# Turning x instead of its outer product, and loading the spherical rows repeated over the partitions, in a two-layer graph kernel

## The reference, cut to what matters

```python
def tensor_product(x_e, sh, w, C):
    # out[e,o] = w[e,o] * sum_{d,s} x_e[e,d] * sh[e,s] * C[d,s,o]
    acc = sh[:, 0:1] * (x_e @ C[:, 0, :])
    for s in range(1, S):
        acc = acc + sh[:, s:s + 1] * (x_e @ C[:, s, :])
    return acc * w
k = tensor_product(x_dst, edge_sh, wk, Cqk).reshape(-1, H, DQK)
v = tensor_product(x_dst, edge_sh, wv, Cv).reshape(-1, H, DV)
attn = jnp.einsum('ehd,ehd->eh', q[edge_src], k)
# softmax of attn over the edges of a node, then the weighted sum of v
```

## Time and profile before

| | |
|---|---|
| median of 3 runs | 3733.17 us |
| profiled execution | 3729.88 us, span 3728.2 us |
| PE / PEld busy | 3330.0 us (89%) / 3178.9 us (85%) |
| DVE busy | 2877.5 us (77%) |
| POOL busy | 2055.4 us (55%) |
| ACT busy | 1285.0 us (34%) |
| DMA queues q1, q0, q10 | 44.2%, 9.7%, 4.1% of 16 engines' span |

### The profile page before, as it was taken

One profiled execution on the slowest core, in us unless ns is written; L12 is line 12 of the kernel. 1 busy time (PEld: TensorE's weight loads), 2 busy tenths in 40 slices (PEclk: granted clock), 3 DMA queues, 4 the chain that ended last, 5 costly groups with the idle time before them and its releaser, 6 DMA issues. The chain is left out here.

```text
span 3728.2 us, 86642 instructions
## 1 busy us (share of the span) xinstructions
PE 3330.0 (89%) x25947; PEld 3178.9 (85%) x25947; DVE 2877.5 (77%) x5292; ACT 1285.0 (34%) x3333; POOL 2055.4 (55%) x1999
## 2 busy tenths in 40 slices
PE   2099999999999337999999999999999999999963
PEld 1088888888888237999999999999999999999953
DVE  4366666666666227999999999999999999999943
ACT  1033333333333113444444444444444444444420
POOL 2577777777777435555555555555555555555540
PEclk9599999999999658999999999999999999999975
DMA  8399999999999313444444444444444444444420
GB/s 339 86 268 280 279 279 279 279 280 279 279 280 279 105 46 105 127 126 132 131 124 129 131 129 124 130 132 126 125 132 132 124 128 131 130 124 129 132 78 29
DMA packets 843789, 622.16 MB, mean 167 GB/s; under 512 B 490431, under 2 KB 732803, under 8 KB 843452
## 3 DMA queue, kind: packets, MB, share of 16 engines
q1 hardware_dynamic: 667110, 500.09, 44.2%
q0 software_dynamic: 56640, 87.65, 9.7%
q10 hardware_dynamic: 119982, 33.79, 4.1%
HBM read 335.87 MB, written 286.31 MB: 167 GB/s over the span
## 5 line engine op out<-in xcount | busy, mean ns | idle before, releaser
L1305 POOL DMA_INDIRECT xg<-h_tab,src_i x808 | 861.5, 1066 | 220.8 <-issue 127.2
L789 POOL DMA_INDIRECT kv<-kv_tab,src_i x808 | 762.1, 943 | 285.7 <-issue 188.2
L1315 POOL TENSOR_TENSOR kq<-kvs,q_of 128x512 f32<-128x512 f32 x202 | 260.6, 1290 | 837.7 <-DVE kvs L1491 837.7
L1401 ACT ACTIVATE z_hi<-bank 128x512 fp32r<-128x512 f32 x808 | 439.4, 595 | 802.9 <-PE bank L1333 802.9
L1357 PE MATMUL bank<-C_hi,z_hi 128*128 128x256 f32 x4040 | 682.2, 299 | 0.0
L1357 PE MATMUL bank<-C_lo,z_hi 128*128 128x256 f32 x4040 | 612.2, 281 | 0.0
L1481 DVE TENSOR_TENSOR z_lo<-bank,z_hi 128x512 fp32r<-128x512 f32 x808 | 520.5, 686 | 113.5 <-ACT z_hi L1401 113.4
L1357 PEld LDWEIGHTS bank<-C_hi,z_hi 128*128 128x128 f32 x4040 | 537.8, 191 | 0.3
L1357 PEld LDWEIGHTS bank<-C_lo,z_hi 128*128 128x128 f32 x4040 | 535.3, 188 | 0.0
L1357 PE MATMUL bank<-C_hi,z_lo 128*128 128x256 f32 x3232 | 516.2, 281 | 0.0
L913 DVE TENSOR_TENSOR wsb<-bank,b 128x512 f32<-128x512 f32 x404 | 279.3, 691 | 298.7 <-PE bank L977 298.3
(11 more groups left out here) (248 smaller groups left out, 4754.4 us busy)
## 6 DMA issues: line engine op xcount, KB each, us to landing
w_tab<-wsb SPq DMA_DIRECT2D x202, 512.0 KB, 3.4
win<-w_tab SPq DMA_DIRECT2D x202, 512.0 KB, 3.6
sum_edge<-rowt SPq DMA_DIRECT2D x202, 288.0 KB, 2.5
q_edge<-zq SPq DMA_DIRECT2D x202, 256.0 KB
qs<-q_edge SPq DMA_DIRECT2D x202, 256.0 KB, 2.8
sum_edge<-rows ACTq DMA_DIRECT2D x202, 136.0 KB
qs<-q_edge SPq DMA_DIRECT2D x202, 128.0 KB
drow<-dst_tab SPq DMA_DIRECT2D x202, 128.0 KB, 3.2
```

Source lines behind the costliest of these rows:

```text
L789: pool.indirect_dma_start(kv[b][:, q, :], None, kv0_tab, bass.IndirectOffsetOnAxis(ap=src_i[:, i * Q + q:i * Q + q + 1], axis=0))\
L1305: pool.indirect_dma_start(xg[b][:, q, :], None, h1_tab, bass.IndirectOffsetOnAxis(ap=src_i[:, i * Q + q:i * Q + q + 1], axis=0))\
L1315: pool.tensor_tensor(kq[:, :].rearrange("p (q o) -> p q o", q=Q), kvs[b][:, :, 0:O1], q_of[b % 2][:, :].rearrange("p (q o) -> p q o", q=Q) ...
L1401: nc.scalar.activation(z_hi[b % 2][:, k, :], bank[ZB[k]][:, :], ACT.Copy).then_inc(hi_out, 1)
```

## The change

z is formed with features on partitions from the start. POOL gathers x as before; PE turns x alone (2 transposes per chunk instead of 18); ACT copies it to `xT`, where partitions 0 to 63 and 64 to 127 both hold the 64 features of all 512 edges. Since z then lies with (s,d) on partitions, sh must lie as one row of 512 edges for each s, repeated over 64 partitions. The middle phase therefore makes two tables, `sh_tab` (202 chunks x 8 x 512) and `sh_last_tab` (202 x 512), and in the second pass a DMA loads a chunk's rows repeated: 128 partitions with 8 KB each. Of the four pairs of sh, DVE multiplies three (one instruction of 1536 columns) and POOL the fourth (`z_part`). ACT and DVE then make `z_hi` and `z_lo` from SBUF in pieces of 1024 columns. `spread_q` gets a PSUM bank of its own.

```diff
             with nc.Block() as block:      # middle phase
+            SG = NST // 2                  # 101
+            sh_rows = [sb(f"sh_rows{g}", [SG, ST, S], F32, ph) for g in range(2)]
+            sh_parts = sb("sh_parts", [SG, S, ST], F32, ph)
                 def _(sp):
+                    def load_sh_rows(a):
+                        last_full = (NST - 1) * ST
+                        sp.dma_start(sh_rows[0][:, :, :], a[0:SG * ST, :].rearrange("(p e) s -> p e s", p=SG))\
+                          .then_inc(sh_rows_in, 16)
+                        sp.dma_start(sh_rows[1][0:NST - 1 - SG, :, :],
+                                     a[SG * ST:last_full, :].rearrange("(p e) s -> p e s", e=ST)).then_inc(sh_rows_in, 16)
+                        sp.dma_start(sh_rows[1][NST - 1 - SG:NST - SG, 0:TAIL, :], a[last_full:E, :].unsqueeze(0))\
+                          .then_inc(sh_rows_in, 16)
                     load_last_rows(sp, lrows, sum0_edge, last_got)
+                    with sp.If(flag > 0):
+                        load_sh_rows(ea9_s)
+                    with sp.Else():
+                        load_sh_rows(ea9)
...
                     sp.dma_start(car[:, :, :], ...).then_inc(car_got, 16)
+                    for g in range(2):
+                        sp.wait_ge(sh_parts_set, g + 1)
+                        sp.dma_start(sh_tab[g * SG:(g + 1) * SG], sh_parts[:, 0:S - 1, :]).then_inc(sh_put, 16)
+                        sp.dma_start(sh_last_tab[g * SG:(g + 1) * SG, :], sh_parts[:, S - 1, :]).then_inc(sh_put, 16)
                     sp.wait_ge(h1_ready, 1)
...
                 def _(act):                # after the copies to crows, ahead of those to wvT
+                    act.wait_ge(sh_rows_in, 48)
+                    for g in range(2):
+                        if g:
+                            act.wait_ge(sh_put, 32)
+                        for r in range(2):
+                            nc.scalar.activation(sh_parts[:, 4 * r:4 * r + 4, :],
+                                                 sh_rows[g][:, :, r:S - 1:2].rearrange("p e c -> p c e"), ACT.Copy)
+                        nc.scalar.activation(sh_parts[:, S - 1, :], sh_rows[g][:, :, S - 1], ACT.Copy)\
+                                 .then_inc(sh_parts_set, 1)
...
                     def load_sh(it, i, b):       # second pass, SP
-                        need(sp, z_ready, (i - RING + 1) * 2)
-                        load_either(sp, sh_turn, flag, i, sh[b][:, :, :], ea9, ea9_s, sh_in[b], sh_tail)
+                        need(sp, z_last_ready, i - 1)
+                        sp.dma_start(sh_last[b % 2][:, :], sh_last_tab[bass.ds(i, 1), :].rearrange(
+                            "a (r e) -> (a r) e", r=2).unsqueeze(1).broadcast_to([2, D, ST // 2])).then_inc(sh_in[b % 2], 16)
+                        need(sp, z_part_ready, i - 1)
+                        sp.dma_start(sh[b % 2][:, :, :].rearrange("p c e -> p (c e)"),
+                                     sh_tab[bass.ds(i, 1)].rearrange("a (r c) e -> (a r) (c e)", r=2)
+                                     .unsqueeze(1).broadcast_to([2, D, 4 * ST])).then_inc(sh_in[b % 2], 16)
...
+                    def z_part(it, i, b):        # POOL
+                        pool.wait_ge(x_out, i + 1)
+                        pool.wait_ge(sh_in[b % 2], 32 * (2 * it + b // 2 + 1))
+                        need(pool, lo_out, i * 3 - 4)
+                        pool.tensor_tensor(z[b % 2][:, ZD, :], xT[b % 2][:, :], sh[b % 2][:, ZD, :], ALU.mult)\
+                            .then_inc(z_part_ready, 1)
-                    unrolled([(times_q, -1), (gather_x, 4)], RING)
+                    unrolled([(times_q, -1), (z_part, 2), (gather_x, 5)], RING)
...
-                    pipelined(pe, [(t_z(0), 1), (t_z(1), 1), (turn_max, -2), (sums, -3), (m_acc(0), 0), (t_z(2), 1),
-                                   (t_z(3), 1), (m_acc(1), 0), (t_z(4), 1), (spread_q, 0), (m_acc(2), 0),
-                                   (turn_logits, -1), (m_acc(3), 0)], RING)
+                    pipelined(pe, [(turn_x, 3), (turn_max, -2), (sums, -3), (m_acc(0), 0), (m_acc(1), 0), (turn_logits, -1),
+                                   (spread_q, 0), (m_acc(2), 0), (m_acc(3), 0)], RING)
...
+                    def outer(it, i, b):         # DVE
+                        dve.wait_ge(x_out, i + 1)
+                        dve.wait_ge(sh_in[b % 2], 32 * (2 * it + b // 2 + 1))
+                        need(dve, lo_out, i * 3 - 4)
+                        dve.tensor_tensor(z[b % 2][:, 0:ZD, :], bcast(xT[b % 2][:, :], 1, ZD), sh[b % 2][:, 0:ZD, :],
+                                          ALU.mult).then_inc(z_ready, 1)
...
-                    pipelined(dve, [(product(1), -1), (lo(0), 1), (lo(1), 1), (subtract, -2), (outer(0), 2), (lo(2), 1),
-                                    (lo(3), 1), (logits, -1), (weigh, -2), (outer(1), 2), (lo(4), 1), (build, 1),
-                                    (segment_max, -1), (product(0), 0)], RING)
+                    pipelined(dve, [(product(1), -1), (subtract, -2), (outer, 2), (logits, -1), (weigh, -2), (lo(0), 1),
+                                    (lo(1), 1), (outer_last, 2), (build, 1), (lo_last, 1), (segment_max, -1),
+                                    (product(0), 0)], RING)
```

More of the change, by code:

```diff
@@ L1111, in _ @@
                     sp.wait_ge(tab3, 16)
+                    sp.wait_ge(sh_put, 64)
                     sp.wait_ge(carry_zero, 16 * 9)
@@ L1212, in gnn @@
             RING = 4
-            sh = [sb(f"sh{b}", [P, Q, S], F32, ph) for b in range(RING)]
+            sh = [sb(f"sh{b}", [P, 4, ST], F32, ph) for b in range(2)]
+            sh_last = [sb(f"sh_last{b}", [P, ST // 2], F32, ph) for b in range(2)]
+            xT = [sb(f"xT{b}", [P, ST], F32, ph) for b in range(2)]
             xg = [sb(f"xg{b}", [P, Q, D], F32, ph) for b in range(RING)]
@@ L1403, in stage @@
[L1403 to L1408 removed]
+                            nc.scalar.activation(z_hi[b % 2][:, 2 * k:2 * k + 2, :], z[b % 2][:, 2 * k:2 * k + 2, :],
+                                                 ACT.Copy).then_inc(hi_out, 1)
@@ L1409, in take_q, with hi_last @@
+                        return stage
+                    def hi_last(it, i, b):
+                        act.wait_ge(z_last_ready, i + 1)
+                        need(act, a_mm, i * 2 - 2)
+                        for f, e in zip(rows_of, edges_of):
+                            ins = nc.scalar.activation(z_hi[b % 2][f, 4, e], z_last[b % 2][f, :], ACT.Copy)
+                        ins.then_inc(hi_out, 1)
                     def take_q(it, i, b):
@@ new lines, in outer, with outer_last @@
+                    def outer(it, i, b):
[4 more added lines that the diff above has]
+                                          ALU.mult).then_inc(z_ready, 1)
+                    def outer_last(it, i, b):
+                        need(dve, lo_out, i * 3 - 3)
+                        for f, e in zip(rows_of, edges_of):
+                            ins = dve.tensor_tensor(z_last[b % 2][f, :], xT[b % 2][f, e], sh_last[b % 2][f, :], ALU.mult)
+                        ins.then_inc(z_last_ready, 1)
@@ L1481, in stage, with lo_last @@
-                            dve.tensor_tensor(z_lo[b % 2][:, k, :], bank[ZB[k]][:, :], z_hi[b % 2][:, k, :].bitcast(F32),
+                            c = slice(2 * k, 2 * k + 2)
+                            dve.tensor_tensor(z_lo[b % 2][:, c, :], z[b % 2][:, c, :], z_hi[b % 2][:, c, :].bitcast(F32),
                                               ALU.subtract).then_inc(lo_out, 1)
                         return stage
+                    def lo_last(it, i, b):
+                        dve.wait_ge(hi_out, i * 3 + 3)
+                        need(dve, a_mm, i * 2 - 2)
+                        for r in range(2):
+                            f, g, e = rows_of[r], rows_of[1 - r], edges_of[r]
+                            ins = dve.tensor_tensor(z_hi[b % 2][g, 4, e], z_last[b % 2][f, :],
+                                                    z_hi[b % 2][f, 4, e].bitcast(F32), ALU.subtract)
+                        ins.then_inc(lo_out, 1)
```

127 lines of the change are left out of this document (52 added, 75 removed).

## The result

The changed kernel takes 7142.83 us (median of 4 runs, 7138.11 to 7144.25) where the kernel before, run beside it, takes 3733.63 us (4 runs, 3731.1 to 3735.28): a ratio of 1.913, 95% interval 1.9097 to 1.9163. The forecast was 7240 us.

What follows compares the result with a forecast made beforehand. The prediction took the load of sh on two DMA engines, 27.4 us per chunk, to bound the second pass. 3729.9 + 16 + 3371 + 15 + 130 = 7262 us, forecast as 7240 us, range 6880 to 7700.

Steps and rivals of the forecast that it cites:

- The count of engines: Load of sh: engines are the largest number up to 16 dividing both sides' outer size, here two.
- The step: Second pass: sh packets plus a share of other transfers on two engines take 27.4 us per chunk; 201 steps, +3371 us.
- the rest of the queue: Second pass: each of the two engines also carries its sixteenth of other transfers, q1's 3.6 us and q0's 0.5.
- My doubt: Load of sh: an 8 KB packet read again and again may cost other than one read once, priced at 318 ns.
- Everything else hidden under it: Second pass: the two engines never run dry, so PE, DVE (9.7 us), POOL and ACT hide under them.
- The ends of the pass: Second pass: +16 us until the first outer product, and +15 us for the tail, from between 0 and 27.
- The middle phase: Table building: DMAs of 101 rows, a prime, run on one engine and delay ACT's wvT to about 1429; +130 us.
- the upper bound: Middle phase: strided reads double ACT's copies, making it +140 us.
- The sum: Whole kernel: 3729.9 + 16 + 3371 + 15 + 130 = 7262 us; 7240 forecast for packets at their lower price.
- Rival 1: Second pass: load spread over 16 engines, GpSimd and VectorE block each other; step 11.65 us, 4070 us; chance 0.06.
- Rival 2: Second pass: load spread over 16 engines, no blocking of long instructions; DVE bounds at 9.7 us, about 3545 us; chance 0.04.
- rival 3: Second pass: two engines per load, but successive loads take different pairs; 16 us a step, 4960 us; chance 0.04.

Runs made afterwards that it cites:

- distinct: dup_x, but the two sh loads read 64 differing rows of 8 KB each instead of one row 64 times; 3676.82 us, ratio 0.985 to the kernel before.
- mid_only: The kernel before with only the changed kernel's middle phase added, its tables written but never read; 3867.53 us, ratio 1.036.
- halves: The changed kernel with each load of sh and sh_last cut into two DMAs of 64 partitions; 4021.51 us, ratio 1.077 to the kernel before.
- z_on_dve: halves_mid with GpSimd's product z_part given to VectorE, as one outer product of 2048 columns; 3913.81 us.
- psum_x: z_on_dve with the outer product reading x from PSUM, table and gather holding x twice, ACT's copies dropped; 3728.29 us, ratio 0.9969 to the kernel before.
- halves_mid: halves with the middle phase in groups of 112 and 90 chunks instead of twice 101; 3896.44 us.
- dup_x: psum_x with gathers of 64 numbers again, ACT doubling the gathered rows in SBUF; 3683.9 us, ratio 0.985 to the kernel before.

## Why the prediction was right, step by step

**The count of engines.** Right, and the step on which all else hung. The completions show two engines for sh and two for sh_last, and in the variants 2, 3, 7 and 16. The Trainium skill ("DMA: Bandwidth & Descriptors", section "Why a DMA increments its semaphore by 16 and not by 1") has this rule; by it every count in the table comes out, and the trace agrees in all six. For the load of sh alone it shows in its 8 KB packets, of which two are under way at once and hardly ever three.

**The step: 27.4 us forecast, 26.83 measured.** The sum was 0.57 us too long, which makes 114 us over 201 steps. Which term that belongs to depends on how the 8 KB packet is counted. It was put at 318 ns, drawn from packets of 6400 and 14400 bytes. Its median is 309: 64 of these are 0.58 us less, and the rest of the queue, 3.6 + 0.5 = 4.1 us, is what the measured step then leaves (26.83 - 19.78 - 2.94 = 4.11). Its mean is 321, near the forecast, and then the rest was over-priced, with 3.35 us left for it. The trace doesn't name the engines, so it doesn't decide between the two. The 1 KB packet is 46 ns in the median, as worked out. My doubt that a packet that is read again and again has another price is answered by these 309 ns, which lie under what rows read once had suggested, and for sixteen engines by `distinct`.

**Everything else hidden under it.** Right. PE, VectorE, GpSimd and ACT each end in the wait for sh, and as far as the packets tell the two engines never ran dry: from the tenth to the ninetieth in a hundred the steps lie between 26.6 and 27.1 us. The granted clock was 0.69 and not the 0.5 that I allowed for.

**The ends of the pass.** 16 + 15 us forecast, 19.1 - 1.9 measured. The tail's 15 was the middle of a range of 0 to 27 and should have been its lower end; why it costs nothing was not looked into.

**The middle phase: +130 forecast, +134.0 measured**, and the same +134.0 alone in `mid_only`. Within it the load landed at 1332.6 (I had 1327), and ACT's two large copies took 7.54 us instead of 3.7: the doubling that I had put into the upper bound was what happened. The first store still kept its dates, because `car` and the zeros stood before it on its engine: its first packet is at 1353.9 us (I had 1350), and ACT goes on behind it and its companion at 1423.6 (I had 1423). `wvT` came 3 us later than 1429, by ACT's longer second copies.

**The sum.** 7262 us was added up and 7240 named, for packets at their lower price. The profiled run is 7138, 124 under the sum: 114 in the steps, 14 at the ends, and 4 the other way in the middle phase. No large errors cancelled.

**Rival 1**, had the load been spread, said 11.65 us a step and 4070 us. `halves` is that case: 11.37 and 4021.5. The wait for logits was priced at 1.3 us and is 1.2; `va`'s at 0.65 and is 0.45. **Rival 2** (9.7 us, no blocking) and **rival 3** (other pairs for successive loads) are excluded, the one by z_on_dve and psum_x, the other by steps of 26.83 and not 16 us and by the two packets under way. The Trainium skill ("SBUF — State Buffer", section "Who interferes with whom") speaks of an exclusive lock between a VectorE instruction with two SBUF inputs and GpSimd's reads; k x q at 2.83 us beside such an instruction and at 1.30 beside one that reads PSUM agrees with it.

## What to carry to other kernels

Before a broadcast load or a layout of tables is chosen, write down the outermost size on both sides of the DMA and the largest number up to 16 that divides both: in every kernel here that many engines carried it, and when they were too few, the rest of the queue waited for them. A mean DMA share tells nothing of this; the time of one packet times the packets per engine does, and so does the count of completion packets. Once that is right, look at which of VectorE's long instructions have both inputs in SBUF while GpSimd computes, and at how near the DMA engines' work per step is to the step.

## What I had not expected of the hardware

- The queue's issue itself takes longer when engines are behind. With one engine behind by two large DMAs, SP's nine stores of zeros took 61.55 us to issue instead of 9.31, and `mask` 7.51 us instead of 0.69. SP was late for DMAs whose data has nothing to do with the large load. Even those 9.31 us show it: the first four stores are issued in 0.29 to 0.59 us each, the last three in 1.67 to 1.96, near the 1.8 us that the prediction works out for one store on its five engines. How much an engine can have in its queue before SP is held was not tried.
- Long instructions exclude each other in both directions. In the changed kernel, where both start together when sh lands, VectorE's outer product of 1536 columns takes 2.8 us in 158 of 202 steps, and `z_part` then its own 1.3. In the other 44 it is the other way round: the outer product takes 1.76 us and `z_part` 2.8 to 2.9. In the long ones the outer product starts 5 to 67 ns behind `z_part`, in the others 4 or 5 ns behind or 17 to 44 ns ahead of it. So it is always one of the two that waits for the other, and who comes first decides, as far as starts 5 ns apart can tell. The averages are 2598 ns (1739 in halves_mid) and 1612:

```profile
L1509 DVE TENSOR_TENSOR z<-xT,sh 128x1536 f32<-128x1536 f32 x202 | 524.9, 2598 | 3243.1 <-DMA sh<-sh_tab 3044.7 <-issue 198.4
L1368 POOL TENSOR_TENSOR z<-xT,sh 128x512 f32<-128x512 f32 x202 | 325.7, 1612 | 2962.8 <-issue 2936.3 <-DMA sh<-sh_tab 26.5
```

- An 8 KB packet takes 309 ns while two engines carry the large load and 570 to 590 with sixteen. So by these prices spreading a load over eight times the engines makes it less than five times as fast, and near a mean share of one the time scatters by some per cent from run to run (3655 to 3747 us for dup_x, where the kernel before stays within 3730 to 3738). Which part of the memory path sets this was not tried.
- ACT's copy that reads every second of nine numbers takes 3.77 us for 2048 columns, twice what its rate in the earlier trace rows gives.
